# Loading the adjacency matrix by row groups over all 128 partitions instead of by quadrants of 32

## The reference

```python
h = relu(layernorm(x))
terms = [h, adj @ h]                              # Chebyshev terms, K = 4
terms += [2 * (adj @ terms[-1]) - terms[-2]]      # twice
x = x + einsum('kni,kio->no', stack(terms), weight)
h = relu(layernorm(x))
deg = clip(sum(adj, axis=1) + 1, 1)
h_neigh = (adj @ h + h) / deg
out = relu(concat([h, h_neigh], 1) @ W + b)
return x + out / max(norm(out), 1e-12)
```

## Time and profile before

| | |
|---|---|
| time, median of 3 runs | 2661.69 us |
| time of the profiled execution | 2672.75 us |
| its span | 2670.9 us |
| mean granted TensorE clock | 0.92 of 2.4 GHz |
| moved by the DMA engines | 689.56 MB, 258 GB/s |
| busy: PE, DVE, POOL, ACT | 81%, 61%, 31%, 27% |

### The profile page before, as it was taken

The page is one execution under the profiler, slowest core; times in us unless marked ns, Lnnn a source line. Parts: engine busy times, 40 slices in busy tenths (PEclk is TensorE's granted clock), DMA queues, the critical chain, the costliest instruction groups (busy, mean ns, idle before and its releaser), DMA issues.

```text
span 2670.9 us, 20670 instructions
## 1 busy us (share of the span) xinstructions
PE 2152.7 (81%) x6792; PEld 919.9 (34%) x6792; DVE 1637.1 (61%) x1204; ACT 730.2 (27%) x2243; POOL 821.6 (31%) x1521
## 2 busy tenths in 40 slices
PE   0567778888999999989988979889886897776666
PEld 0123233333334444444434434333332343222222
DVE  2755556656656565756564566766575655576766
ACT  1766666666676674000000000000000000000000
POOL 2222223222322323323222434233232332233423
PEclk9988989999999999999999999889998998888878
DMA  9999999999999999999999999999999999999994
GB/s 206 259 261 265 274 262 268 274 270 268 269 277 276 266 262 258 234 272 238 265 248 259 252 261 257 268 250 269 276 254 268 264 272 267 271 264 270 248 258 127
DMA packets 326445, 689.56 MB, mean 258 GB/s; under 512 B 56514, under 2 KB 93378, under 8 KB 326338
## 3 DMA queue, kind: packets, MB, share of 16 engines
q1 hardware_dynamic: 216832, 344.03, 56.8%
q0 software_dynamic: 108672, 344.03, 46.1%
q10 hardware_dynamic: 834, 0.20, 0.0%
HBM read 685.97 MB, written 2.10 MB: 258 GB/s over the span
## 4 chain that ended last, share of the span: by engine, by line
PE 30%; DMA 29%; SPq 28%; ACT 5%; DVE 5%; issue 2%; POOL 0%; DVEq 0%; ACTq 0%
DMA ring<-in_adj_dram 28%; SPq L317 27%; PE ps_pair L745 23%; ACT ring L393 5%; PE ps_single L751 4%; DVE ring L601 3%; SPq L306 1%; DMA res<-in_x_dram 1%; PE ps_lin L690 0%; PE ps_lin L693 0%; PE ps_lin L706 0%; PE ps_tr L709 0%; PE ps_lin L698 0%; PE ps_xt L642 0%; PE ps_single L652 0%
## 5 line engine op out<-in xcount | busy, mean ns | idle before, releaser
L601 DVE STREAM_TRANSPOSE ring<-ring 128x2048 f32<-128x2048 f32 x640 | 1431.6, 2284 | 810.2 <-DMA ring<-in_adj_dram 536.6
L745 PE MATMUL ps_pair<-ring,vec 128*128 128x512 f32 x2880 | 1319.3, 616 | 151.8 <-DVE ring L601 140.4
L351 POOL DMA_DIRECT2D ring<-in_adj_dram x1448 | 786.0, 551 | 1811.9 <-PE ps_pair L745 1131.1
L745 PEld LDWEIGHTS ps_pair<-ring,vec 128*128 128x128 f32 x2880 | 559.4, 198 | 878.6 <-issue 766.5
L751 PE MATMUL ps_single<-ring,vec 128*64 128x512 f32 x2240 | 591.1, 665 | 285.2 <-DVE ring L601 281.2
L393 ACT ACTIVATE ring<-ring 128x512 f32<-128x512 f32 x1024 | 628.0, 615 | 297.3 <-DMA ring<-in_adj_dram 297.3
L751 PEld LDWEIGHTS ps_single<-ring,vec 128*64 128x64 f32 x2240 | 159.6, 149 | 644.9 <-issue 423.9
L420 ACT ACTIVATE sum_s<-ps_single 128x512 f32<-128x512 f32 x64 | 37.7, 590 | 616.7 <-PE ps_pair L745 449.5
L393 ACT ACTIVATION_READ_ACCUMULATOR ring<-ring 128x1 f32 x1024 | 192.0, 188 | 0.0
L422 ACT ACTIVATE sum_p<-ps_pair 128x512 f32<-128x512 f32 x45 | 26.6, 591 | 452.2 <-PE ps_pair L745 452.2
L431 ACT ACTIVATE stat<-stat 128x4 f32<-128x4 f32 x16 | 3.3, 205 | 258.7 <-DVE stat L554 258.7
(11 more groups left out here) (95 smaller groups left out, 576.7 us busy)
## 6 DMA issues: line engine op xcount, KB each, us to landing
ring<-in_adj_dram POOLq DMA_DIRECT2D x1160, 256.0 KB, 12.1
ring<-in_adj_dram SPq DMA_DIRECT2D x1160, 256.0 KB, 18.4
ring<-in_adj_dram POOLq DMA_DIRECT2D x96, 192.0 KB, 11.2
ring<-in_adj_dram SPq DMA_DIRECT2D x96, 192.0 KB, 18.6
ring<-in_adj_dram POOLq DMA_DIRECT2D x96, 128.0 KB, 10.9
ring<-in_adj_dram SPq DMA_DIRECT2D x96, 128.0 KB, 13.9
ring<-in_adj_dram SPq DMA_DIRECT2D x96, 64.0 KB, 15.2
ring<-in_adj_dram POOLq DMA_DIRECT2D x96, 64.0 KB, 10.2
```

What stands on the lines that cost most here:

```text
L351: pool.dma_start(dst, src).then_inc(s_high[i % NSEM], 16)
L601: nc.vector.transpose(blocks, blocks).then_inc(s_turned, 1)
L745: last = nc.tensor.matmul(ps_pair[n % 2][:], vec[:, CB * J + c, :, :], moving, start=(k == pair_at[0] and c == 0), stop=(k == pair_at[-1] ...
```

## The change

The same bytes go to the same places of the ring in the same number of DMAs of the same size. A DMA now covers one row group over all four column quarters. SP issues the eight even groups and POOL the eight odd ones. On the side of DRAM such a DMA walks column quarter a (4 of them, 8 KB apart), then row r (32 of them, 32 KB apart), then the contiguous run of columns. On the side of the ring it walks 128 partitions with one contiguous run each. The two sets of semaphores are renamed, and their counts stay.

```diff
-    adj_v = adj.rearrange("(a c r) m -> a r c m", a=Q, r=32)
+    adj_v = adj.rearrange("(b c r) (a m) -> b c a r m", b=Q, r=32, a=Q)
...
-                for ar in range(Q):
-                    for a in (0, 1):
-                        col = a * QN + J0 * UC
-                        src = adj_v[ar, :, CB * row.C:CB * row.C + CB, col:col + w * UC]
-                        dst = strip_of(i)[32 * a:32 * a + 32, ar:G:Q, :]
-                        sp.dma_start(dst, src).then_inc(s_low[i % NSEM], 16)
+                for g in range(0, G, 2):
+                    src = adj_v[g % Q, CB * rows[n].C + g // Q, :, :, J0 * UC:J0 * UC + w * UC]
+                    sp.dma_start(strip_of(i)[:, g, :], src).then_inc(s_even[i % NSEM], 16)
...
-                for ar in range(Q):
-                    for a in (2, 3):
-                        col = a * QN + J0 * UC
-                        src = adj_v[ar, :, CB * row.C:CB * row.C + CB, col:col + w * UC]
-                        dst = strip_of(i)[32 * a:32 * a + 32, ar:G:Q, :]
-                        pool.dma_start(dst, src).then_inc(s_high[i % NSEM], 16)
+                for g in range(1, G, 2):
+                    src = adj_v[g % Q, CB * rows[n].C + g // Q, :, :, J0 * UC:J0 * UC + w * UC]
+                    pool.dma_start(strip_of(i)[:, g, :], src).then_inc(s_odd[i % NSEM], 16)
```

More of the change, by code:

```diff
@@ L276, in cheb_sage_kernel @@
         s_wready = sem("weights_ready")
-        s_low = [sem(f"strip_low_loaded{i}") for i in range(NSEM)]
-        s_high = [sem(f"strip_high_loaded{i}") for i in range(NSEM)]
+        s_even = [sem(f"strip_even_loaded{i}") for i in range(NSEM)]
+        s_odd = [sem(f"strip_odd_loaded{i}") for i in range(NSEM)]
         s_turned = sem("units_turned")
@@ L386, in sum_rows @@
                     return
-                act.wait_ge(s_low[i % NSEM], 8 * Q * Q * (i // NSEM + 1))
-                act.wait_ge(s_high[i % NSEM], 8 * Q * Q * (i // NSEM + 1))
+                act.wait_ge(s_even[i % NSEM], 8 * Q * Q * (i // NSEM + 1))
+                act.wait_ge(s_odd[i % NSEM], 8 * Q * Q * (i // NSEM + 1))
                 if C >= 2:
@@ L584, in _ @@
             for i, (n, J0, w, units) in enumerate(strips):
-                dve.wait_ge(s_low[i % NSEM], 8 * Q * Q * (i // NSEM + 1))
-                dve.wait_ge(s_high[i % NSEM], 8 * Q * Q * (i // NSEM + 1))
+                dve.wait_ge(s_even[i % NSEM], 8 * Q * Q * (i // NSEM + 1))
+                dve.wait_ge(s_odd[i % NSEM], 8 * Q * Q * (i // NSEM + 1))
                 if rows[n].sweep == 1:
```

## The result

The changed kernel takes 5507.67 us (median of 4 runs, 5457.28 to 5544.36) against 2661.85 us; the ratio is 2.0623 with a 95% interval of 2.0428 to 2.0818. One of its four runs, 5544.36 us, is counted as slow, and the ratio is that of the three others. The profiled execution took 5536.91 us, with a span of 5535.1 us. Forecast were 4850 us and a range of 4200 to 6750.

A forecast was written before the change was run, and what follows sets the result against it. Loads bound the kernel, SP's half being late. On SP's four engines, 107.0 MB each at 22.4 GB/s gave 4777 us, with 46 and 35 us at the ends 4858; forecast 4850 us, range 4200 to 6750.

The forecast's parts named there:

- The spread: Engines per load: outermost counts 4 and 128 allow 4 engines, not 16; q1 falls from 216832 to 199456 packets.
- The same four engines for SP: SP's queue takes the same four engines each time, 85.5 MB of its loads on each; case given 0.82.
- POOL's turns: POOL's software-made DMAs go round the engines in turn, so each engine gets a sixteenth, 21.5 MB.
- The rate of one engine: One busy DMA engine taken at 22.4 GB/s, bounds 16.1 slow and 26.4 fast.
- The sum: 107.0 MB per SP engine at 22.4 GB/s, 4777 us, plus start and end: 4858 us.
- both ends: 46 us until SP's first load of `adj` and some 35 us after the last loads land.
- POOL's sixteenth: A sixteenth of POOL's 344.03 MB, 21.5 MB, on each of SP's four engines; 960 us at 22.4 GB/s.
- less crowded: Four busy engines mean less total traffic than in any row, so 22.4 GB/s, near the uncrowded end.
- What hides behind it: TensorE's 7 to 13 us and DVE's 10 us a strip stay covered by a strip every 29 us.
- The rival of the faster side: Rival (a): all engines share the work, SP alone loses its 210 GB/s limit; 2450 us, 8% faster; chance 0.10.
- Its 328 GB/s: Skill's rate for all 128 partitions; would make rival (a)'s sum an estimated 2170 us, at which TensorE would bind.

The follow-up runs named there:

- SP's quadrants: Changed kernel with SP's even groups loaded by quadrants of 32 partitions, POOL's loads as in the changed kernel: 3289.59 us, ratio 1.2373.

## Why the prediction was right

**The spread: right, and to the packet.** 199456 was forecast for q1 and measured, and the count moves back with the source's outermost index alone. It was shown for 4 against 32, not for other counts.

**The same four engines for SP: right.** The full four show as 24.9% of 16 in each pause. The evidence is the share, not the engines' numbers, which the profile doesn't give.

**POOL's turns: right.** Its share of 55.1% with SP's quadrants shows that it isn't held to four engines, and the turns could even be used up.

**The rate of one engine: wrong in both directions, with one error hiding part of the other.** The sum took 22.4 GB/s for all bytes on the four engines. For SP's own 85.5 MB that gave 3817 us; with POOL left out, the stream took 3505 less the 81 us of both ends, 3424 us, or 25.0 GB/s. For POOL's sixteenth it gave 960 us; POOL's loads cost 2030. The balance is -393 + 1070 = 677 us, and 4858 + 677 is the span of 5535 us. The mis-sized term is POOL's: I priced its bytes on SP's engines, not what its traffic on all engines does to SP's packets, though I had read the earlier trace rows as two engines getting in each other's way. That the sum came within 14% of the span is in part luck, as the 393 us too many for SP's own bytes stood against the 1070 too few. I had argued that four busy engines would be less crowded. That is true in the pauses, and in a burst it isn't.

**What hides behind it: right.** TensorE is busy for 43% of the span, at a granted clock of 0.71 of 2.4 GHz where it had 0.92, so it was more often at 1.2 GHz, and it stayed covered: PE has 5% of the chain.

**The rival of the faster side** had nearly the right price for what it described: 2450 us, and 2316 us were measured where all 16 engines share each load. It did not come about because of the 4. The rule of the Trainium skill cited there (SBUF — State Buffer, "Door 1: The DMA port swizzle") agrees in direction: full 128-partition loads raise slices from at most 277 to 364 GB/s. Its 328 GB/s were an estimate of 2170 us, which lies on the low side as TensorE binds. The Trainium skill's rule on the number of engines (DMA: Bandwidth & Descriptors, "Why a DMA increments its semaphore by 16 and not by 1") now has the case of 4 behind it in this chip's counts.

## What to carry to other kernels

Read the outermost index of both sides of a load before anything else: here a source that began with 4 confined each load to four engines, and on SP's queue always the same ones. The packets of SP's queue tell it without a timeline, since there each engine that takes part posts once; on POOL's queue the posts stay at 16 for a load, and the short packets of the next section show it. When one queue's half is late, look at which partitions are written while it works alone; a third queue for part of its loads gained 7.7% here, where a reshaping of them lost 106%.

## What the runs showed of the hardware that was not expected

POOL's queue sends more packets for a load on four engines. In the new shape q0 has 357504 packets, of which 1512 x 16 = 24192 are posts and 1024 I take for the stores (64 of 32 KB, at 2 KB a packet). The other 332288 are exactly 4 x 83072, so each packet with data has three short ones beside it, of 8 to 32 bytes in the packet records, and the queue moved 2.22 MB more. SP's queue has no such packets. It looks as if they stand for the twelve engines that the load doesn't use, but the records name no engine.

Packets of both queues take longer in company. In the changed kernel POOL's hold 35.4% of 16 engines over 5535 us, 31.3 ms of engine time, against 19.7 ms before (46.1% of 2670.9 us), for the same data and the short packets. SP's hold only 17.5 ms against 24.3, because it is alone for much of the time: one of its packets, posts included, takes 24.9% x 16 x 12 us / 583 = 82 ns in the pause and 12.3% x 16 x 11 us / 124 = 175 ns in the burst.
